# Logits and the turning back of z move ahead of the first attention products on TensorE

## The reference

```
mod = (_silu(L0_c) @ L0_wmod).reshape(L0_c.shape[0], 6, 1, -1)
sa, ca, ga, sb, cb, gb = (mod[:, 0], mod[:, 1], mod[:, 2], mod[:, 3], mod[:, 4], mod[:, 5])
...
h = _layernorm(x, axis=-1) * (1 + ca) + sa
    # attention of h:
    K = jnp.exp(_linear(x, Wk1, bk1))
    K_cum = jnp.cumsum(K, axis=1) + 1e-06
    S = jnp.cumsum(K * V, axis=1) / K_cum
    Q = jax.nn.sigmoid(_linear(x, Wq1, bq1))
    O_ar = S * Q
    E = jnp.concatenate([zero, V[:, 1:, :] - O_ar[:, :-1, :]], axis=1)
    S2 = jnp.cumsum(K2 * E, axis=1)
    O_ma = S2 * Q2
    return _linear(O_ar + O_ma, Wproj, bproj)
x = x + ga * attention
h = _layernorm(x, axis=-1) * (1 + cb) + sb
    # experts of h:
    logits = x.astype(jnp.float32) @ centroids.astype(jnp.float32).T
    assign = jnp.argmax(logits, axis=-1)
    ...  # layernorm with the expert's own gain and bias, then W1, relu, W2, plus the token itself
x = x + gb * experts
```

## Time and profile before

| | us |
|---|---|
| median of 3 runs | 346.22 |
| lowest and highest | 344.87, 346.59 |
| the profiled execution | 343.75 |
| its span in the trace | 342.0 |

### The profile page before, as it was taken

How to read it: one execution, slowest core, us unless ns; L and a number is a source line. 1 busy time by engine, 2 the same in 40 slices (tenths; PEclk the granted TensorE clock), 3 DMA queues, 4 the chain that set the end, 5 groups by cost and what they waited for, 6 DMA issues and landing times.

```text
span 342.0 us, 8121 instructions
## 1 busy us (share of the span) xinstructions
PE 293.8 (86%) x1853; PEld 228.6 (67%) x1853; DVE 267.7 (78%) x921; ACT 248.6 (73%) x555; POOL 236.4 (69%) x370
## 2 busy tenths in 40 slices
PE   8588878998989899899678999999999989999910
PEld 7335445664655655565377999999999978888810
DVE  6898999999999989799775686996685666766540
ACT  2868989999898989989858666776677666666400
POOL 7984275668988787878558878878887735445460
PEclk9959999999999999999999999999999999999985
DMA  7333288436469887643487889778877777785000
GB/s 215 86 99 93 74 255 217 110 104 174 151 193 203 213 207 176 91 137 141 135 268 216 281 286 317 229 232 228 224 233 207 208 226 240 222 224 156 31 16 0
DMA packets 49429, 60.86 MB, mean 178 GB/s; under 512 B 5557, under 2 KB 38095, under 8 KB 49379
## 3 DMA queue, kind: packets, MB, share of 16 engines
q1 hardware_dynamic: 42806, 43.11, 48.2%
q0 software_dynamic: 6368, 16.82, 13.7%
q10 hardware_dynamic: 208, 0.41, 0.3%
HBM read 39.90 MB, written 20.87 MB: 178 GB/s over the span
## 4 chain that ended last, share of the span: by engine, by line
PE 52%; DVE 14%; issue 11%; ACT 8%; DMA 4%; POOL 3%; SPq 3%; ACTq 2%; DVEq 1%; POOLq 0%
PE bank L817 12%; PE bank L790 11%; DVE shared L1192 3%; PE bank L794 3%; PE bank L742 3%; PE bank L718 3%; PE bank L721 3%; PE bank L733 3%; PE bank L759 3%; PE bank L669 2%; ACT shared L916 2%; PE bank L692 2%; ACT shared L1019 2%; DMA x_in<-expert_rows 2%; PE bank L769 2%
## 5 line engine op out<-in xcount | busy, mean ns | idle before, releaser
L591 POOL DMA_INDIRECT out_dram<-shared,ids x71 | 73.1, 1029 | 41.2 <-DVE shared L1645 24.0
L516 POOL DMA_INDIRECT expert_rows<-rows,slots x64 | 64.6, 1009 | 17.4 <-issue 15.5
L817 PE MATMUL bank<-w_all,shared 128*128 x568 | 69.5, 276 | 1.5 <-DVE shared L1442 1.5
L817 PEld LDWEIGHTS bank<-w_all,shared 128*128 128x128 f32 x568 | 66.3, 192 | 1.9 <-issue 1.9
L1011 ACT ACTIVATE shared<-bank,par 128x256 f32<-128x256 f32 x100 | 41.0, 470 | 23.8 <-PE bank L790 23.7
L790 PE MATMUL bank<-shared,early 128*128 128x256 f32 x200 | 47.6, 381 | 1.2 <-ACT shared L1011 1.2
L479 POOL TENSOR_SCALAR zz<-rows,negm,rstd 128x128 f32<-128x128 f32 x64 | 32.0, 510 | 23.9 <-ACT rstd L993 18.6
L790 PEld LDWEIGHTS bank<-shared,early 128*128 128x128 f32 x200 | 36.1, 191 | 5.2 <-issue 1.3
L1459 DVE TENSOR_TENSOR shared<-bank,b_bc 128x256 f32<-128x256 f32 (+1 forms) x46 | 15.8, 362 | 30.3 <-PE bank L817 20.5
L471 POOL TENSOR_SCALAR xh<-x_in,negm,rstd 128x128 f32<-128x128 f32 x64 | 29.6, 472 | 7.1 <-DVE shared L1165 6.7
L1034 ACT ACTIVATE shared<-bank,par 128x256 f32<-128x256 f32 (+1 forms) x46 | 22.6, 513 | 8.2 <-issue 4.9
(11 more groups left out here) (212 smaller groups left out, 678.0 us busy)
## 6 DMA issues: line engine op xcount, KB each, us to landing
early<-in_L_ffn_W_dram SPq DMA_DIRECT2D x25, 256.0 KB
x_in<-expert_rows SPq DMA_DIRECT2D x15, 385.0 KB, 4.0
rows<-in_L_ffn_W_dram SPq DMA_DIRECT2D x21, 256.0 KB
x_in<-in_L_attn_x_dram SPq DMA_DIRECT2D x16, 256.0 KB, 3.2
rows<-gates_rows SPq DMA_DIRECT2D x32, 128.0 KB, 5.1
full<-expert_rows SPq DMA_DIRECT2D x10, 385.0 KB, 4.4
expert_rows<-pad_rows SPq DMA_DIRECT2D x9, 385.0 KB, 8.9
full<-expert_rows SPq DMA_DIRECT2D x11, 192.5 KB, 3.1
```

The lines of the kernel that those rows point to most:

```text
L516: pool.indirect_dma_start(rows_dram, bass.IndirectOffsetOnAxis(ap=slots[:, c * CN + t:c * CN + t + 1], axis=0), rows[:, c % RR, t, :], Non ...
L591: pool.indirect_dma_start(out_rows, bass.IndirectOffsetOnAxis(ap=ids[:, u % IR, t:t + 1], axis=0), u_sb[:, k, t, :], None, bounds_check=T - 1,
L817: mm = pe.matmul((ps_q, ps_k)[k][:, t * D:(t + 1) * D], hid[:, k, f, t * P:(t + 1) * P], of_expert(w2_all, e, f * D, (f + 1) * D), start=( ...
```

## The change

`logits(z)` and `turn_back(z)` are called ahead of the wait for `Oar` and the four products with it, instead of behind them. No instruction is added or removed.

```
                               start=False, stop=False)
+                if in_a(z):
+                    logits(z)
+                    turn_back(z)
+                if in_a(c):
                     pe.wait_ge(s_Oar, c + 1)
                     pe.wait_ge(s_wg, c + 1)
                     for t in range(CN):
                         s, l = t * P // L, t * P % L
                         pe.matmul(ps_proj[:, t * P:(t + 1) * P], Oar[:, c % 2, s, l:l + P], wg[:, CS * c + s, :],
                                   start=False, stop=False)
-                if in_a(z):
-                    logits(z)
-                    turn_back(z)
```

## The result

Eight timed runs of the changed kernel have a median of 342.54 us (339.08 to 343.73), eight of the kernel before 346.03 (344.20 to 350.35). The ratio is 0.9875 with a 95% interval of 0.9836 to 0.9914: 1.25% faster, about 4.3 us, where I had said 2.5. It leaves out slow executions, those over 1.5% above the fastest of the same kernel (here the one of 350.35), so it differs a little from the medians, which lie 3.5 apart. The direction and the mechanism were right.

The account below looks back on a forecast made before the run. No single engine bounds the first phase; TensorE and VectorE delay each other at semaphores. Even steps give −2.56 us, the h2T wait costs 0.1, so about −2.5 from 346.22 makes 343.7 us; range 342.6 to 346.4.

Parts of the forecast that it names:

- Logits earlier: First phase: logits start 0.99 us earlier, ending VectorE's wait in steps 4, 6, 8, 10 and 0.99 of step 12's.
- The new wait for h2T: TensorE before the logits: h2T is no longer covered by the Oar products; 0.04 us to spare, cost 0.1 in all.
- Products with Oar later, z back earlier: First phase: Oar products start 1.28 us later at cost 0; ScalarE gets the turned-back h2T earlier at gain 0.
- What an earlier S2 is worth: Even steps 4 to 12: TensorE can give 0.56 us each, step 6 only 0.32; 2.56 in all.
- ScalarE's cap: Even steps: ScalarE's 0.67 us wait for the transposed x limits the gain to about 0.63 per step.
- Whether it gets to the end: Start of second phase, through GpSimd's scatters: all 2.56 us pass, or 2.00 at the low end; everything behind only moves.
- the 0.80 in front of the first scatter: GpSimd, step 13: delay from slots to first scatter; 2.56 us pass if it answers to the slots, otherwise 2.00.
- The lead didn't leak away: Rival, first phase: a second engine takes up part of the gain, leaving −1.3 to −2.0 us; 344.9 us, chance 0.14.
- The first weights weren't exposed: Rival, TensorE: the logits' first weight load loses cover, 0.11 to 0.12 us in 13 steps; 345.2 us, chance 0.09.
- h2T wasn't late at the head of the queue: Rival, slower: TensorE stalls after the shift product for ScalarE's h2T, 0.35 us in 13 steps; 348.3 us, chance 0.09.
- GpSimd was not the pacer: Rival, no effect: GpSimd paces the second phase's start, so the gain is 0 to 1 us; 345.8 us, chance 0.11.
- the marks that I named: Signs in the changed trace: shorter waits, later Oar products, step 12 at 137.3, expert-row load at 164.3, second phase 160.2 us.

Follow-up runs that it names:

- The late copy: The changed kernel with one more 128 by 128 copy on ScalarE ahead of h2T; median 377.4 us, ratio to the kernel before 0.997.
- the odd steps alone: The kernel before with logits and turning back moved ahead only in odd steps; median 379.6 us, ratio to the kernel before 1.010.
- routing late: The kernel before with VectorE's routing moved behind S2, TensorE's order kept; median 376.3 us, ratio to the kernel before 0.999.
- the four on chip 6: Kernel before (378.5 us), same with an added ScalarE copy ahead of h2T (378.0), changed kernel with one tanh halved (364.8), changed kernel without the shift product (373.3).

## Why the prediction was right in kind and too small in size

1. *Logits earlier.* Right. The waits in steps 4, 6, 8 and 10 are gone, and one of 0.76 is left of the 1.62 in step 12; I had left 0.63.

2. *The new wait for h2T.* Right, at the low end. I had put 0.1 on it; the logits stand 0.31 behind the shift product, as their predecessor did, so nothing is visible. The late copy shows how near it was: 0.22 more of ScalarE and the even steps pay 0.21.

3. *Products with Oar later, z back earlier.* Right, both nothing. The keys (L711) start 2.59 us behind the shift product (L735) in step 8 of both kernels, and the kernel with the logits alone ahead shows the second.

4. *What an earlier S2 is worth.* This step failed, in its size. I took 0.56 per step, 0.48 of printed idle time in front of L718 and 0.08 behind it, under a cap of 0.63 at ScalarE. It was 0.89 to 0.91 in steps 8, 10 and 12. The idle time of the profile runs from the modelled end of one instruction to the start of the next. Products that are ready start before their predecessor's end: L718 now starts 0.86 behind L711, whose duration is printed as 1.02. From start to start the gap was 1.51 − 0.86 = 0.65 and not 0.48, the next 1.10 − 0.86 = 0.24 and not 0.08. This spacing stood in the trace of the kernel before, in step 9, where nothing holds the three products:

```profile
113.85 1.02 PE L711 MATMUL bank<-shared,wT 128*128 128x512 f32 x2
114.71 1.02 PE L718 MATMUL bank<-shared,wT 128*128 128x512 f32 x2
```

ScalarE's cap was short in the same way. Its idle time was 0.67, but from the tanh at L937 to that at L940 there are 0.57 now (104.78 to 105.35), and in the kernel before 0.71 to the row of 106.74:

```profile
106.03 0.65 ACT L937 ACTIVATE bank<-bank,bias 128x512 f32<-128x512 f32 x1
```

That is 0.14 more, and hT now starts 0.09 before the last tanh ends (105.93 against 106.02): 0.67 + 0.14 + 0.09 = 0.90. With 0.9 as the cap the sum would have been 0.63 + 0.32 + 3 × 0.9 = 3.65, and 3.73 came out; that is worked out after the fact. The idle time printed for VectorE was short too, by the same kind of overlap. From the start of the gated error to that of the largest logit, steps 4, 6, 8, 10 and 12 took 1.30, 0.92, 1.49, 1.54 and 2.29 us before and take 0.59, 0.58, 0.59, 0.68 and 1.43 now. The differences, 0.71, 0.34, 0.90, 0.86 and 0.86, are within 0.07 of what the steps gained (0.73, 0.41, 0.91, 0.89, 0.90). So in step 4, for which I had 0.56, and in step 6, for which I had 0.32, the gain follows VectorE's wait; and TensorE's, VectorE's and ScalarE's reckonings for step 8 come to the same 0.9, so that the runs don't tell which of them caps it. The rest of the sum stood.

5. *Whether it gets to the end.* Right as to GpSimd: with the whole lead of step 13 (3.89) the load of expert rows moved by 3.87, so the 0.80 in front of the first scatter did answer to the slots. That all of it passed has some luck in it: the first scatter of step 13, held by GpSimd's own copy now, kept only 3.68, and a shorter normalisation gave the 0.2 back. Behind it I took everything as "moved, not changed", and there the profiled execution lost 1.35 us by the first expert product, 1.14 of it on TensorE while the clock was at its lower level. That loss is no part of the change: the kernel before has its like in one of its two profiles.

6. *The rivals.* The lead didn't leak away: the odd steps kept their length to 0.04, and the even ones gave more than the cap. The first weights weren't exposed, h2T wasn't late at the head of the queue, and GpSimd was not the pacer. Of the marks that I named, two missed, by 1.0 and 1.4: step 12 started at 136.26 and not 137.3, and the load came at 162.94 and not 164.3, both for the same reason, the gain per step. The wait of L718 for S2 is gone in steps 4, 8 and 10, so is ScalarE's in front of the transposed x, the products with Oar start 1.38 us later behind L735, and the second phase takes 160.36, as I had said.

## What to carry to other kernels

Where an instruction of a pipelined engine waits in one trace, price the wait from start to start against the closest spacing that the same instructions show elsewhere, not by the idle time printed in front: here 0.56 became 0.9 per step, and the closest spacing could be read from a neighbouring step of the same trace. A wait of VectorE for TensorE and one of TensorE for VectorE in the same step may be one event counted twice; taking it away from either side gives all of it, and doing both gives nothing more. Once it is gone, ask by small added delays, rather than by busy shares, what bounds next: in the changed kernel 0.22 us put in front of h2T cost 0.21 in steps 8 and 10, while a product taken from TensorE, busy 9.41 of 9.41 us there, gave nothing. And before a run is read as an answer, see in its trace that the edit had run when the thing to be explained happened.

## What the runs showed of the hardware that was not expected

- The granted clock fell to its lower level between the phases in some executions of either kernel, and at differing places (from about 173 us in the changed kernel on the first chip, from about 171 on chip 8, from about 178 in the kernel before on chip 6). What TensorE had done before it doesn't set them apart here: 4.1 us busy of 6 in front of one fall, 4.4 in the kernel before, which had none there. The second tile then came 1.1 to 1.8 us later, and in one kernel with a short fall 0.2. Why one execution has it and another not stays open.
- The other chips ran the first phase at about the speed of the first (96.97 and 96.95 us for the changed kernel, 101.26 and 100.68 for the one before) and the whole 34 us slower (380 and 346). In the traces the difference begins between 180 and 240 us. The changed kernel has TensorE busy for 39.3 of these 60 us on chip 8 and for 59.7 on the first chip, and there ScalarE (L1012) and VectorE (L1460) stand still for up to 9 us at a time, released by nothing that the profile knows. It moves the same 60.86 MB. The cause wasn't looked for.
- In 7 of the 12 profiles on the other chips, all of them on chips 14 and 8, ScalarE stands still for 1.55 to 1.77 us at one and the same instruction of step 13, released by nothing that the profile knows; in the changed kernel this is

```profile
155.02 0.66 ACT L934 ACTIVATE bank<-bank,bias 128x512 f32<-128x512 f32 x1 [1.75 <-remote]
```

It comes behind step 13's start and so outside the way that I measure. The changed kernel on the first chip hasn't got it, nor have the kernel before, the odd steps alone, and the four on chip 6; routing late has it (1.66), with TensorE's old order. So it goes neither with the change nor with every profile of a chip. What releases ScalarE there was not found.
